# Four of the token-spreading copies of a mixture-of-experts layer move from ScalarE to GpSimd

## The reference

```python
x = x + attn(layernorm(x))          # k, v, q projected, Fourier-transformed; real part of ifft(cumsum(k*v) * conj(q) / norm)
x = x + xattn(layernorm(x), ctx)    # 16 heads of 64, causal, ALiBi, softmax, Wo
x = x + ffn(layernorm(x))           # two Kronecker mixture layers with an exact gelu between them

def kmoe(x_flat, W_router, A, B, scale, bias, ...):   # x_flat: 64 tokens of 1024 per batch
    vals, idx = top_k(x_flat @ W_router.T, 2)         # 64 experts, 2 taken
    probs = softmax(vals)
    Y = einsum('nkoi,nij,nkpj->nkop', A[idx], x_flat.reshape(-1, 32, 32), B[idx])
    return einsum('nkop,nk->nop', Y, probs).reshape(...) * scale + bias
```

## Time and profile before

| | |
|---|---|
| median of three runs | 1346.33 us (1343.77 to 1350.6) |
| the profiled execution's own time | 1348.9 us |
| its span | 1347.1 us |
| TensorE busy | 1216.1 us, 90% |
| ScalarE busy | 1077.5 us, 80% |
| VectorE busy | 957.9 us, 71% |
| GpSimd busy | 596.6 us, 44% |

### The profile page before, as it was taken

How to read it: one execution, slowest core, us unless ns; L and a number is a source line. 1 busy time by engine, 2 the same in 40 slices (tenths; PEclk the granted TensorE clock), 3 DMA queues, 4 the chain that set the end, 5 groups by cost and what they waited for, 6 DMA issues and landing times.

```text
span 1347.1 us, 51835 instructions
## 1 busy us (share of the span) xinstructions
PE 1216.1 (90%) x16466; PEld 974.0 (72%) x16466; DVE 957.9 (71%) x3651; ACT 1077.5 (80%) x3126; POOL 596.6 (44%) x1870
## 2 busy tenths in 40 slices
PE   6799999999999999999999999999999999987534
PEld 5667687877777787777778787777778787765423
DVE  1365779695968879695978779596878879594514
ACT  2456899898988899898989899798989889887441
POOL 3122446362645446363645546263545536252513
PEclk9999999999999999999999999999999999998555
DMA  9200101010100101010010101010010101010000
GB/s 290 42 17 10 33 15 42 12 42 18 35 25 17 36 17 42 12 40 20 27 33 16 37 15 41 14 39 21 19 42 10 42 12 41 8 30 15 25 18 9
DMA packets 67745, 43.09 MB, mean 32 GB/s; under 512 B 18577, under 2 KB 66322, under 8 KB 67218
## 3 DMA queue, kind: packets, MB, share of 16 engines
q1 hardware_dynamic: 67474, 39.77, 10.6%
HBM read 35.51 MB, written 4.19 MB: 29 GB/s over the span
## 4 chain that ended last, share of the span: by engine, by line
PE 54%; DVE 16%; SPq 10%; issue 10%; ACT 3%; DMA 2%; POOL 2%; DVEq 1%; POOLq 1%; ACTq 0%
SPq L419 9%; PE P L738 5%; PE X L796 4%; PE P L706 4%; PE PT L761 4%; PE P L717 4%; PE PT L796 4%; PE P L695 3%; DVE own L1061 3%; PE F L875 3%; PE X L783 3%; PE F L900 3%; DVE chosen_dn L360 3%; PE S L754 3%; PE G L835 2%
## 5 line engine op out<-in xcount | busy, mean ns | idle before, releaser
L360 POOL COPY chosen_dn<-experts 64x64 f32 x1024 | 224.5, 275 | 225.7 <-issue 160.4
L598 ACT ACTIVATE probs<-probs,neg_max 128x128 f32<-128x128 f32 (+1 forms) x512 | 226.4, 444 | 24.3 <-DVE neg_max L1020 20.7
L346 POOL COPY chosen_up<-experts 32x128 f32 x512 | 182.4, 356 | 105.6 <-POOL chosen_up L346 51.2
L346 ACT COPY chosen_up<-experts 32x128 f32 x512 | 151.3, 296 | 25.1 <-PE G L881 11.2
L1020 DVE CUSTOM_DVE_ANT_0 probs<-S,distance 128x128 f32<-128x128 f32 (+1 forms) x512 | 151.8, 350 | 13.8 <-PE S L754 10.3
L761 PE MATMUL PT<-ident,probs 128*128 128x128 f32 x768 | 136.2, 287 | 10.1 <-DVE probs L1038 5.7
L637 ACT ACTIVATE hT<-h 64x1024 f32<-64x1024 f32 x64 | 126.7, 1980 | 15.3 <-DVE h L1151 13.9
L1038 DVE TENSOR_TENSOR probs<-probs,rinv 128x768 f32<-128x768 f32 x128 | 128.7, 1006 | 4.4
L875 PE MATMUL F<-chosen_up,own 64*64 64x64 f32 x2048 | 91.1, 230 | 38.6 <-DMA chosen_up<-in_experts_up 25.9
L875 PEld LDWEIGHTS F<-chosen_up,own 64*64 64x64 f32 x2048 | 76.9, 141 | 66.7 <-issue 55.1
L706 PE MATMUL P<-ctxT,wk 128*128 128x256 f32 x512 | 122.1, 382 | 2.1 <-DVE x L998 2.1
(11 more groups left out here) (130 smaller groups left out, 2858.4 us busy)
## 6 DMA issues: line engine op xcount, KB each, us to landing
chosen_up<-in_experts_up SPq DMA_DIRECT2D x1024, 16.0 KB, 1.6
x<-in_x SPq DMA_DIRECT2D x16, 256.0 KB, 2.7
ctxT<-in_ctxT SPq DMA_DIRECT2D x16, 256.0 KB, 3.1
out<-x2b SPq DMA_DIRECT2D x16, 256.0 KB, 2.3
experts<-in_experts_up SPq DMA_DIRECT2D x2, 1024.0 KB, 19.9
wk<-in_xWk SPq DMA_DIRECT2D x1, 1024.0 KB
wo<-in_xWo SPq DMA_DIRECT2D x1, 1024.0 KB
wv<-in_xWv SPq DMA_DIRECT2D x1, 1024.0 KB, 7.7
```

What stands on the lines that cost most here:

```text
L346: last = copy(to[row:row + D1, n * 2 * F1:(n + 1) * 2 * F1], experts_up[k][:, bass.ds(held[g % loaded(units), unit], 2 * F1)])
L360: last = copy(dst, src.rearrange("p (m c) -> p m c", m=2))
L598: act.activation(probs[:, e % 4, lo:hi], probs[:, e % 4, lo:hi], ACT.Exp, bias=neg_max[:, e % 4, rt:rt + 1], scale=-1.0, accum_out=rsum[:, ...
```

## The change

A new step `own_pool@2` is put into `ORDER` between `choose_pool.23@3` and `dn_second.2@3`. GpSimd has a function for it, which writes quadrant 0 with four copies; ScalarE's `own_act` keeps quadrant 1 alone. A semaphore `own_pool` is added. `up.0` waits for four counts of ScalarE, four of GpSimd and eight of VectorE in each batch. `ln3_keep`, which overwrites `xn3T`, also waits until GpSimd's copies of the batch before are done.

```diff
-choose_sync.7@2 f_keep.1 v.1@1 turn_a.2@1 pv.1@1 choose_pool.23@3 dn_second.2@3 choose_act.23@3 choose_pool.0@2
+choose_sync.7@2 f_keep.1 v.1@1 turn_a.2@1 pv.1@1 choose_pool.23@3 own_pool@2 dn_second.2@3 choose_act.23@3 choose_pool.0@2
...
+            def spread_tokens(c):
+                wait_f(pool, "ln3_turn", None, c)
+                pool.wait_ge(zeroed, 1 + DN_SLOTS)
+                after(pool, first_done[0], at(c, UP_PAIRS, 0))
+                for il in range(4):
+                    pool.tensor_copy(*own_parts(0, il)).then_inc(own_pool, 1)
...
             def ln3_keep(c):
                 act.wait_ge(xn3_turned, at(c, 1, 1))
                 after(act, own_dve, at(c, 8, 0))
+                after(act, own_pool, at(c, 4, 0))
...
-                for n in (0, 1):
-                    for il in range(4):
-                        act.copy(*own_parts(n, il)).then_inc(own_act, 1)
+                for il in range(4):
+                    act.copy(*own_parts(1, il)).then_inc(own_act, 1)
...
                     if v == 0:
-                        pe.wait_ge(own_act, at(c, 8, 8))
+                        pe.wait_ge(own_act, at(c, 4, 4))
+                        pe.wait_ge(own_pool, at(c, 4, 4))
                         pe.wait_ge(own_dve, at(c, 8, 8))
```

More of the change, by code:

```diff
@@ L266, in decoder_layer @@
         pv_done, pair_kept, wo_done = sem("pv_done"), sem("pair_kept"), sem("wo_done")
-        xn3_turned, own_act, own_dve = sem("xn3_turned"), sem("own_act"), sem("own_dve")
+        xn3_turned, own_act, own_dve, own_pool = sem("xn3_turned"), sem("own_act"), sem("own_dve"), sem("own_pool")
         chosen = {name: [sem(f"chosen_{name}_up"), sem(f"chosen_{name}_dn")] for name in CHOOSERS}
@@ L524, in choose @@
                     pool.wait_ge(chosen["pool"][1], at(c, DN_GROUPS, n - UP_GROUPS + 1))
-            run({"choose_pool": choose,
+            def spread_tokens(c):
[4 more added lines that the diff above has]
+                    pool.tensor_copy(*own_parts(0, il)).then_inc(own_pool, 1)
+            run({"choose_pool": choose, "own_pool": spread_tokens,
                  "x1_bias": bias_x1, "x2_bias": bias_x2, "cross": cross, "lane": lane, "root": fpower_root,
```

## The result

The changed kernel takes 1352.82 us (median of 11 runs, 1349.91 to 1356.86), the kernel before 1345.99 us in its 11 runs: ratio 1.0055, 95% interval [1.0041, 1.0069]; the medians are 6.8 us apart. The ratios in this text are estimates that leave out the few executions at a far lower granted clock, and not quotients of two medians, so the two can differ by about 0.1%. Run once more on another occasion it gave 1.0053 [1.0032, 1.0073], and the kernel before against itself 1.0000 [0.9984, 1.0015]. The profiled execution took 1352.3 us, with a span of 1350.6 us.

What follows compares the result with a forecast made beforehand. TensorE was taken to bound the middle turns, with a few short stalls. Hindrance of VectorE (+4.9 us), the last turn (+0.85) and the first (-0.4) summed to +5.4 us, giving 1351.7 us from the median; range 1342 to 1364 us.

Steps and rivals of the forecast that it cites:

- ScalarE's relief is worth 0 in a middle turn: ScalarE's 2.6 us a turn would end in its idle time of 0.82 us for VectorE's masks, gaining about 0.
- The 0.4 us of the first turn: In the first spreading turn TensorE waits 0.41 us for `catch_a` behind `own_act`; a gain of 0.4 us once.
- GpSimd's price: Each of GpSimd's four 32x256 stepped copies would take 0.60 us, between bounds of 0.387 and 0.757.
- VectorE's copies are hindered and TensorE waits for it: GpSimd overlaps VectorE's spreading copies by 0.46 us; half to all delays TensorE at `dn_weigh.3`: 0.35 us a turn, +4.9 us.
- The last turn: In the last spreading turn GpSimd and VectorE's copies overlap 1.7 us; half, +0.85 us, reaches TensorE's wait for W_dn.
- `lane.0` is covered: GpSimd's idle time of 4.40 us before `lane.0` absorbs the 2.4 us put back, shrinking to about 2.0 us.
- The sum: Middle turns +4.9 us, last turn +0.85, first turn -0.4: in all +5.4 us, 1351.7 us from the median.
- rival 1: GpSimd's copies cost 0.5 us or less and end before VectorE begins; ScalarE's gain vanishes; 1346 us; chance 32%.
- Rival 3: GpSimd is much slower: from 1.1 us a copy `lane.0` comes late too; at 1.3 us about 1371 us and up; chance 11%.
- TensorE's waits for ScalarE fewer: Sign named as showing the forecast wrong: fewer TensorE waits for ScalarE, which were 5.5 us for `chosen_up`.
- The chances: Faster 0.10, within 0.5% 0.59, slower 0.31, before shifting 0.04 from the middle to slower.

Runs made afterwards that it cites:

- the run with GpSimd's copies alone: The kernel before, ScalarE keeping all eight copies, plus GpSimd's four copies at the change's place into a tile nobody reads; ratio 1.0055.
- The short copies: The kernel before plus four GpSimd copies of 256 neighbouring elements each, at the change's place, into a tile nobody reads; ratio 1.0055.
- the control: The kernel before, unchanged, run once more against itself; ratio 1.0000.
- the split places: GpSimd makes three copies behind `choose_pool.19`, one behind `choose_pool.21`; against the kernel before 1.0096 with ScalarE relieved, 0.9974 with VectorE relieved.

## Why the prediction was right

The direction, the place and the size held: 1351.7 us forecast, 1352.8 measured, in the range of 1342 to 1364. Step by step:

- *ScalarE's relief is worth 0 in a middle turn*: shown, 0.9992 alone. The 0.4 us of the first turn are there: the transpose that waited 0.41 us for `catch_a` starts without a wait.
- *GpSimd's price*: 0.60 us taken, 0.665 measured; bounds 0.387 and 0.757. The factor of 1.77 that ScalarE pays would have given 0.685, the nearest of all. The copies that met none of VectorE's spreading copies took 0.61 to 0.71 us, 0.64 in the middle. By the Trainium skill's "GPSIMD Engine Reference" (Performance pitfalls for Q7 kernels) one cycle more for an element gives an estimate of 0.60 us; the runs show 0.404 us without and 0.665 us with steps, 0.26 us more where that estimate has 0.21.
- *VectorE's copies are hindered and TensorE waits for it*: shown by the run with GpSimd's copies alone. The delay was forecast at 0.35 us a turn and is 0.37 in the turn looked at; W_dn's wait grew by 4.3 us over 13 turns, 0.33 each. But two errors cancel in it, and that is luck: the overlap is 0.95 us, not 0.46, and VectorE loses 0.39 of it, not half to all. The share itself is the wrong measure, in the first turn too: what VectorE loses is what the GpSimd instruction under way still has to run, as the last section shows. By that measure the forecast's own timeline, with 0.46 us left of GpSimd's last copy, gives an estimate of 0.33 us. A reader should not take the half from here.
- *The last turn*: +0.85 us forecast from 1.7 us of overlap; the overlap is 1.31 us, VectorE's copies +0.74 us, TensorE's wait for W_dn 2.46 to 3.56 us.
- *`lane.0` is covered*: 4.40 us to about 2.0 forecast, 1.90 measured.
- *The sum*: +5.4 us forecast, +6.8 measured. Over the whole span the wait for W_dn grew from 16.3 to 22.0 us, 5.7 us; the transposes' wait for VectorE grew by 0.8 us in the middle turns. In exchange `y_turn`'s waits for VectorE, 0.9 us, are gone, and the stretch from `dn_first.0` to `y_turn` itself is 0.28 us longer on average, 3.7 us over 13 turns, and with 1.1 us of the last turn that is some 5 of the 6.8 us. Where the other 2 us arise is not shown.
- *"Nothing is hindered"*, rival 1, was priced wrongly: it says that copies of 0.5 us or less would cost nothing. The short copies of 0.404 us cost 0.55% too, by pushing `cross.0` onto `scale.3`. I had followed GpSimd's put-back work only to `lane.0`'s idle time, and not asked what it would meet on the way.
- *Rival 3*, over 1.1 us a copy, did not occur.
- The named sign "TensorE's waits for ScalarE fewer" as a mark of error was a poor one: they fell from 5.5 to 1.8 us, and the control, the kernel before with 0.9 us, shows that this is chance.
- *The chances*: the points named add to 0.10, 0.60 and 0.30; the text has 0.59 and 0.31. Nothing hangs on it.

## What to carry to other kernels

Before moving work to a less busy engine, ask which engine the bound engine waits for, and relieve that one: in the split places the same four copies make the kernel 0.3% faster or 1.0% slower, by whom they are taken from. Work moved to GpSimd is not free beside a VectorE that has no idle time; follow both the new instructions and every one that they put back, and see which of VectorE's SBUF instructions will begin while one of them is still running: long GpSimd instructions cost there, short ones hardly. Idle time of an engine in a table is room only from the moment when the operands exist, and up to the moment when its next instruction must begin to read its registers.

## What the hardware showed beyond the expected

- Meetings of GpSimd and VectorE cost both sides, and the cost goes by single instructions, not by a share of the overlap. In the changed kernel's turn, VectorE's second spreading copy begins while GpSimd's fourth is under way:

```profile
587.99 0.70 POOL L531 COPY own<-xn3T 32x256 f32<-32x256 f32 x1
588.22 0.73 DVE L1069 COPY own<-xn3T 32x256 f32<-32x256 f32 x1
```

GpSimd's ends at 588.69 and VectorE's 0.26 us later, after 0.73 us; alone it takes 0.39 to 0.40. The trace has 34 spreading copies of VectorE that began when a GpSimd instruction had over 0.15 us left, and each ended 0.25 to 0.28 us after that instruction. The two slow copies of the earlier trace rows, 0.70 and 0.81 us, ended 0.26 us after the two GpSimd operations as well. So such a copy loses what that instruction has left, less about 0.13 us. GpSimd's short `chosen_up` copies of 0.28 to 0.40 us run beside the same VectorE copies and cost next to nothing, since little of them is left. In the other direction, 14 of GpSimd's spreading copies began during one of VectorE's and took about 0.70 us, against 0.64.
- VectorE's `scale`, with two inputs in SBUF, behaves alike. In the kernel with short copies it begins at 594.32, GpSimd's first product ends at 594.71, and `scale` takes 1.21 instead of 0.96 us; GpSimd's second product then ends 0.59 us after `scale` and takes 1.45 instead of 0.72.
- Not every instruction of VectorE is held. `dn_weigh`, with one input in PSUM and one in SBUF, took 0.69 us in all 14 cases of the kernel before in which a GpSimd instruction had over 0.25 us left, as it does alone; the copies from PSUM to `probsT` stayed at 0.56 us in 28.
- The Trainium skill, "SBUF — State Buffer" (Who interferes with whom), has a copy of VectorE in a two-port mode and a GpSimd instruction exclude each other for the whole instruction, and a VectorE instruction with two SBUF inputs collide with one of GpSimd that reads SBUF. The runs agree with both, by the ends 0.25 to 0.28 us apart and by `scale`; in which mode the spreading copies ran, no run shows.
- Reading 32 offsets into registers held GpSimd for 2.25 us that no busy share shows (that it spends them on the registers is read from the kernel; the page says "issue").
- The split of TensorE's waits for a tile with three writers between those writers changes from one execution to the next of the same kernel; their sum was 18.9 and 18.2 us.
